# Attention stage of a gated block written out instead of looped, with another opening, maxima over partitions by TensorE, and earlier weight loads

## The reference

```python
x = x + tanh(g_xattn[0]) * xattn(layernorm(x), ctx, ctx, w_q, w_k, w_v)   # causal, 8 x (1024 x 1024), width 512
x = x + tanh(g_ffn[0])   * ffn(layernorm(x), W1, b1, W2, b2)              # gelu, 512 -> 2048 -> 512
# xattn: softmax(mask((x w_q)(ctx w_k)^T / sqrt(512))) (ctx w_v)
# ffn:   W1 and W2 are ternary: clip(round(w / mean|w|), -1, 1)
```

## Time and profile before

| what | value |
|---|---|
| median of 3 runs | 1773.81 us (1772.19 to 1775.87) |
| profiled execution, own time | 1774.8 us |
| its span in the trace | 1773.0 us |
| PE busy | 1651.3 us (93%) |
| DVE busy | 863.9 us (49%) |
| ACT busy | 658.1 us (37%) |
| POOL busy | 304.0 us (17%) |
| mean granted TensorE clock | 0.97 of 2.4 GHz |

### The profile page before, as it was taken

How to read it: one execution, slowest core, us unless ns; L and a number is a source line. 1 busy time by engine, 2 the same in 40 slices (tenths; PEclk the granted TensorE clock), 3 DMA queues, 4 the chain that set the end, 5 groups by cost and what they waited for, 6 DMA issues and landing times.

```text
span 1773.0 us, 24221 instructions
## 1 busy us (share of the span) xinstructions
PE 1651.3 (93%) x8448; PEld 826.3 (47%) x8448; DVE 863.9 (49%) x1575; ACT 658.1 (37%) x1032; POOL 304.0 (17%) x339
## 2 busy tenths in 40 slices
PE   4699999999999988777699999999999999999999
PEld 1355555565555544433244444444444444444444
DVE  3655656565566554546334434444444444444432
ACT  1223232424233343321244444444444444444443
POOL 1111111111111111111021112211122111221110
PEclk8799999999999998988899999999999999999999
DMA  5245463545545375454322211222112222122210
GB/s 184 71 100 143 98 144 94 138 102 134 104 94 150 90 203 151 131 143 106 82 49 65 66 59 33 61 65 65 59 25 69 65 62 62 24 71 62 64 41 24
DMA packets 261651, 157.52 MB, mean 89 GB/s; under 512 B 222416, under 2 KB 222416, under 8 KB 260432
## 3 DMA queue, kind: packets, MB, share of 16 engines
q1 hardware_dynamic: 261008, 156.31, 34.0%
q10 hardware_dynamic: 576, 0.27, 0.1%
HBM read 70.53 MB, written 33.55 MB: 59 GB/s over the span
## 4 chain that ended last, share of the span: by engine, by line
PE 63%; issue 13%; DVE 12%; DMA 4%; SPq 3%; ACT 3%; POOL 1%; DVEq 0%; POOLq 0%; ACTq 0%
PE t_ps L848 13%; PE e_ps L942 12%; PE s_ps L942 12%; PE v_ps L848 11%; PE o_ps L917 5%; PE s_ps L868 4%; PE t_ps L887 3%; PE v_ps L905 3%; DMA w_in<-in_w1T 2%; SPq L277 2%; DVE v_s L811 2%; DVE cmax L592 2%; DVE negmax L677 1%; ACT p_s L460 1%; DVE w_s L759 1%
## 5 line engine op out<-in xcount | busy, mean ns | idle before, releaser
L785 DVE SCALAR_TENSOR_TENSOR v_s<-g,sc,v_s 128x512 f16<-128x512 f32 x256 | 247.6, 968 | 467.5 <-ACT v_s L517 464.0
L942 PE MATMUL e_ps<-w_s,v_s 128*128 128x512 f16 x1024 | 265.5, 379 | 0.8
L942 PE MATMUL s_ps<-w_s,v_s 128*128 128x512 f16 x1024 | 262.8, 379 | 0.0
L848 PE MATMUL v_ps<-ctx_s,w_s 128*128 128x512 f16 x1024 | 243.6, 381 | 8.9 <-DVE w_s L759 8.9
L848 PE MATMUL t_ps<-ctx_s,w_s 128*128 128x512 f16 x1024 | 243.2, 380 | 0.0
L905 PE MATMUL v_ps<-wv_s,ctx_s 128*128 128x512 f16 x768 | 192.5, 404 | 51.3 <-DVE v_s L719 43.2
L868 PE MATMUL s_ps<-ctx_s,tT 128*128 128x512 f16 (+3 forms) x1152 | 202.3, 331 | 21.4 <-DVE tT L697 14.2
L917 PE MATMUL o_ps<-v_s,pT 128*128 128x512 f16 x864 | 199.9, 383 | 5.0 <-DVE v_s L719 5.0
L887 PE MATMUL t_ps<-xnT,a_s 128*128 128x256 f16 x1536 | 183.5, 277 | 22.6 <-ACT a_s L500 18.6
L517 ACT ACTIVATE v_s<-g,sc 128x512 f16<-128x512 f32 x256 | 184.6, 721 | 8.3
L455 ACT ACTIVATE p<-s_ps,ebias,esc 128x128 f32<-128x128 f32 (+3 forms) x64 | 53.1, 830 | 339.5 <-DVE ebias L683 339.5
(11 more groups left out here) (89 smaller groups left out, 1238.4 us busy)
## 6 DMA issues: line engine op xcount, KB each, us to landing
x_ring<-in_x SPq DMA_DIRECT2D x64, 256.0 KB, 2.8
raw<-in_ctxT SPq DMA_DIRECT2D x8, 2048.0 KB, 8.0
out_y<-x_ring SPq DMA_DIRECT2D x64, 256.0 KB, 2.2
raw<-out_y SPq DMA_DIRECT2D x64, 256.0 KB, 3.2
out_y<-v_s SPq DMA_DIRECT2D x64, 256.0 KB, 2.1
w_in<-in_w1T SPq DMA_DIRECT2D x16, 512.0 KB, 4.3
w_in<-in_w2T SPq DMA_DIRECT2D x16, 512.0 KB, 4.6
xnT<-xn_s SPq DMA_TRANSPOSE x128, 2.5
```

The costliest lines, as they stand in the source:

```text
L785: v.scalar_tensor_tensor(out=g_s[:, f % 4, LO], in0=g32[:, f % 2], scalar=col(C_SG), in1=g_s[:, f % 4, HI], op0=ALU.mult, op1=ALU.subtract ...
L848: last_mm = mm(h_ps[f % 2], w1_s[:, c, (f % FC) * P:(f % FC + 1) * P], yT[:, (f // FC) % 2, a, c, :], start=(a == HI and c == 0), stop=(a ...
L942: last_mm = mm(y_ps[i], g_s[:, f % 4, a, i * P:(i + 1) * P], w2_s[:, f, :], start=(f == 0 and a == HI), stop=(f == FC - 1 and a == LO))
```

## The change

- The `Fori` over three attention turns becomes a Python loop on every engine: 64 slots one behind the other, with no branch. The MLP keeps its loop.
- Maxima and sums over partitions: DVE writes the column of maxima on a diagonal (`ident` times the column, into `dg`), PE multiplies it with ones (`spread_ctx`, a float32 matmul), and DVE reduces the row in PSUM. For the context this matmul stands in PE's slot i = 3, between the scores and T.
- The opening is in another order. Loads go by two queues, A's scale comes from a bound on the weights, known before A is done, PE does ten matmuls ahead of the product, both first T products go to two banks, and the rows of tiles 2 to 4 come later.
- In DVE's slots the lower half of V comes before the output of the tile before, and a second ternary step lies between the two.
- Weight loads of slot t+1 are issued in slot t. `W_PLAN` begins with "SS" and ends sums in slot NT-9, and the sums over partitions move to slots NT-13 and NT-9.
- MLP: four banks for hidden chunks instead of two, PE three chunks ahead. The first three hidden chunks need only W1.

```diff
+            def spread_ctx(batch):
+                pe.wait_ge(ctx_diag, batch + 1)
+                mm(MAXES[:, 0:P], ones[:, :], dg[:, 0], start=True, stop=True).then_inc(ctx_max_all, 1)
...
                     last_mm.then_inc(s_mm, 1)
+                if s > 0 and ctx_step(s) == 3 and (not last or t + TB < NT):
+                    spread_ctx(it * 2 + s // TB + 1)
...
+            def ctx_diagonal(batch):
+                dve.wait_ge(ctx_max, batch + 1)
+                v.scalar_tensor_tensor(out=ccol[:, :], in0=cmax[:, 0:1], scalar=TINY, in1=cmax[:, 1:2],
+                                       op0=ALU.max, op1=ALU.max).then_inc(ctx_col, 1)
+                dve.wait_ge(ctx_col, batch + 1)
+                v.tensor_scalar(dg[:, 0], ident[:, :], ccol[:, :], None, ALU.mult).then_inc(ctx_diag, 1)
...
                         if c == 2:
                             ins.then_inc(ctx_max, 1)
+                            ctx_diagonal(batch)
...
-                if reduce_ctx:
-                    g.partition_all_reduce(call[:, :], cmax[:, :], P, RMAX).then_inc(ctx_max_all, 1)
...
-            with pe.Fori(0, TURNS - 1) as it:
+            for it in range(TURNS - 1):
...
-        W_PLAN = {NT - 15: "SSS", NT - 14: "SSS", NT - 13: "SSS", NT - 12: "SS", NT - 11: "TS", NT - 10: "TS",
-                  NT - 9: "TS", NT - 8: "TS", NT - 7: "TS", NT - 6: "TT", NT - 5: "TT", NT - 4: "TT", NT - 3: "TT",
-                  NT - 2: "TT", NT - 1: "T"}
+        W_PLAN = {NT - 15: "SS", NT - 14: "SSS", NT - 13: "SSS", NT - 12: "TSS", NT - 11: "TSS", NT - 10: "TSS",
+                  NT - 9: "TSS", NT - 8: "T", NT - 7: "T", NT - 6: "T", NT - 5: "T", NT - 4: "TT", NT - 3: "TT",
+                  NT - 2: "TT", NT - 1: "TT"}
...
-                        if at == t:
+                        if at == t + 1:
                             load_weights(m)
...
-                    pe.wait_ge(w_ternary, NW)
+                    pe.wait_ge(w_ternary, NW // 2)
                     hidden(0, 0, 0)
                     hidden(1, 1, 0)
+                    hidden(2, 2, 0)
...
+            t_product(0, -2)
+            t_product(0, -1)
+            spread_ctx(0)
+            v_product(0, -1)
+            slot(0, 0)
```

More of the change, by code:

```diff
@@ L203, in gated_block @@
         PV0 = 2
+        O0 = 1
         def p_turned_by(it, s):
@@ L305, in _ @@
             sp.sem_inc(pv_mm, PV0)
+            sp.sem_inc(o_done, O0)
             sp.sem_inc(y_done, GT)
@@ L432, in _ @@
             a = nc.scalar
+            for c in range(DC):
+                act.dma_start(wqk_in[:, 1, c], wkT[:, c]).then_inc(w_qk_in[c], 16)
+            act.dma_start(wv32, wv).then_inc(w_v_in, 16)
             act.dma_start(col(C_G0), g_xattn.partition_broadcast(P)).then_inc(small_in, 16)
@@ L702, in slot @@
                 for m, n in terns[:1]:
+                    ternary(m, n)
+                if not last or t + 1 < NT:
+                    v_lower(it, s)
+                for m, n in terns[1:]:
                     ternary(m, n)
@@ L738, in slot @@
                                     ALU.add).then_inc(w_total, 1)
-                for m, n in terns[1:]:
-                    ternary(m, n)
             def ternary(m, n):
@@ L826, in _, with product @@
             mm = nc.tensor.matmul
-            def product(c):
-                pe.wait_ge(w_qk_in[c], 32)
-                for m in range(DC):
+            def product(m, cs):
+                for c in cs:
+                    pe.wait_ge(w_qk_in[c], 32)
                     last_mm = mm(a_ps[m], wqk_in[:, 0, c, m * P:(m + 1) * P], wqk_in[:, 1, c, :],
                                  start=(c == 0), stop=(c == DC - 1))
-                    if c == DC - 1 and m % 2:
-                        last_mm.then_inc(a_mm, 1)
+                return last_mm
             def hidden(F, f, g):
@@ L855, in slot @@
                 i = s % TB
-                if s >= 0 and (not last or t < NT):
+                if not last or t < NT:
                     par, pr, q = (s // TB) % 2, (s // 2) % 2, s % 2
@@ L908, in slot @@
+                if not last or t + 1 < NT:
+                    v_product(it, s)
                 if s >= 1:
                     pe.wait_ge(p_turned[(s - 1) % 2], p_turned_by(it, s - 1))
-                    pe.wait_ge(v_split, t + 1 if not last or t < NT else NT)
-                    if last and t == NT:
-                        pe.wait_ge(o_done, NT - 1)
+                    pe.wait_ge(v_split, t)
+                    pe.wait_ge(o_done, t + O0 - 1)
                     jn, par = (s - 1) % TB, ((s - 1) // TB) % 2
@@ L919, in slot @@
                     last_mm.then_inc(pv_mm, 1)
-            for s in range(FIRST_SLOT, 1):
-                slot(0, s)
-                for c in PRODUCTS.get(s, ()):
-                    product(c)
-            with pe.Fori(0, TURNS - 1) as it:
+            pe.wait_ge(consts, 1)
+            for _ in range(WARM):
+                mm(m_ps[:, 0:P], ones[:, :], ones[:, :], start=True, stop=True)
+            for c in range(2):
+                for m in range(DC):
+                    product(m, (c,))
+            for m in range(DC):
+                product(m, (2, 3)).then_inc(a_mm, 1)
+                if m == 0:
+                    pe.wait_ge(a_bound, 1)
+                    mm(BOUND, ones[:, :], wbound[:, :], start=True, stop=True).then_inc(a_bound_all, 1)
+            pe.wait_ge(w_diag, 2)
+            mm(MAXES, ones[:, :], dg[:, :, :].rearrange("p w n -> p (w n)"), start=True,
+               stop=True).then_inc(wmax_all, 1)
+            t_product(0, -2)
+            t_product(0, -1)
+            spread_ctx(0)
+            v_product(0, -1)
+            slot(0, 0)
+            for it in range(TURNS - 1):
                 for s in range(1, BODY + 1):
@@ L934, in group @@
                     F = g * FC + f
-                    if not last or F + 2 < NG * FC:
-                        hidden(F + 2, gg * FC + f + 2, g + (f + 2) // FC)
+                    if not last or F + 3 < NG * FC:
+                        hidden(F + 3, gg * FC + f + 3, g + (f + 3) // FC)
                     pe.wait_ge(g_split, F + 1)
```

374 lines of the change are left out of this document (216 added, 158 removed).

## The result

The changed kernel takes 1701.3 us (median of 4 runs, 1697.72 to 1706.45), and the kernel before takes 1773.0 us beside it (4 runs, 1769.67 to 1775.87). The ratio is 0.9598 [0.9568, 0.9629], so it is faster by 71.7 us. The forecast was 1698 us, in 1658 to 1736. The profiled execution took 1701.67 us, its span is 1699.5 us, and the mean granted clock is 0.985.

What follows compares the result with a forecast made beforehand. PE was taken to bound the MLP and the middle, with the opening and last turn loose. 1774.8 - 74 - 0.5 + 21 - 1 - 7 - 14 = 1699.3, forecast as 1698 us, range 1658 to 1736.

Steps and rivals of the forecast that it cites:

- The last turn, -74: Slot 49's scores to first hidden chunk: waits for weight chunks go, 241.6 us becomes 167.5; bounds -35 and -78.
- the spread's 5.6: In the last turn, the context maximum's spread by TensorE stalls PE once, 5.6 us.
- my 163 to 175: Expected sign: scores of tile 49 to first hidden chunk take 163 to 175 us at clock 0.97 or more.
- The middle, +21 - 1 - 7: Slots up to 48: maximum by TensorE costs five batches +21 us, first batch gains 1, unrolled seams gain 7.
- The 1.4 for POOL's part: In each batch, POOL's reduction no longer delays rows, T and V in slots i = 5 and 6: 1.4 us saved.
- The loop's seams, -7: At 263.54 and 447.01, PE's waits of 2.61 and 2.91 us and 1.3 us of clock go when unrolled.
- The opening, -14: Up to 99.39 us: A's scale known earlier, T waits only for transposed rows; -14 us, bounds -5 and -23.
- The MLP, 0: In the MLP, PE had 5 us of idleness in 902, so four banks bring 0.
- the seam, -0.5: Seam to the MLP: three hidden chunks ahead of the last output instead of two, -0.5 us, bounds -3 and +3.
- the first rival: At the maxima: DVE is early enough, no stall, 1660 us; chance 0.17.
- the second rival: In the last turn: DVE takes over, half of the term goes, +37, 1735 us; chance 0.2.
- the third rival: In the 48 formerly looped slots: straight code must be fetched, 2.6 to 2.9 us each, 1830 us; chance 0.04.

Runs made afterwards that it cites:

- late loads: Changed kernel with each weight load issued again in the slot that uses it: 1765.35 us, ratio 0.9949.
- early loads alone: Kernel before with one edit, the weight loads of slot t+1 issued in slot t: 1722.04 us, ratio 0.97.
- the matmul's new place: Changed kernel with PE's `spread_ctx` moved from ahead of T to behind V in the same slot: 1677.45 us, ratio 0.9439.

## Why the prediction was right, and where its terms were off

The total was 3 us off, and that it was so near is luck in part, because two errors of the sum cancel: the last turn gave 9 us less than its term and the MLP with its seam 7 us more.

- **The last turn, -74.** It was -64.65, inside the bounds. The mechanism is shown from both sides (late loads, early loads alone). The mis-sized step is "I leave 4 us of waits for PE": with the spread's 5.6 that made 9.6 us over the bare work of 157.9, and it was 19.05. PE waited 2.32 us at the spread, 2.17 for the sums, 4.12 for T behind the MLP's rows, 1.01 with no engine named, and 2.81 for the output of tile 62, in sum 12.4, and the rest is mostly slower matmuls behind them. The spread's own share was less than its 5.6, for behind its 2.32 us T took 2.78 and lost no clock. I had looked for what DVE does in its slots, not for what stands in its queue from the next stage. The stage missed my 163 to 175 by 2 us. The second ternary instruction, 1.94 us in the mean against 1.33, some 10 us of DVE in all, was not in my sum either.
- **The middle, +21 - 1 - 7.** It was +13.25 against +13. The stall was right: 3.9 forecast, 3.85 in the mean of the five batches, one of them (4.75) over my upper bound of 4.3. So was its size with clock. A batch of the changed kernel takes 94.57 us and one with no wait 88.6, which makes 6.0 for the wait and its clock, that I had put at 3.9 + 1.5 = 5.4. The matmul itself is in both batches; my 3.9 was "with the matmul" already, so the 0.25 counted it twice. The 1.4 for POOL's part fits too: 90.2 less 88.6 is 1.6. Two edits worked on the stall: the matmul's new place took it away (24 us), and the old place of V's split shortened it (12 us).
- **The loop's seams, -7.** No issue wait was left in the middle. With the loop back the middle took 11.95 us more by the traces, in an execution that is the slowest of its four, and the whole kernel 5.7 to 8.7 us more by the timed runs. The waits themselves are 5.8 of it and the slower scores behind them 1.6. The waits for the diagonal were 1.4 us longer too, 20.6 against 19.3, and the T behind them slower by 1.6; why is open.
- **The opening, -14.** It was -14.96, and T started at 26.75 us, close to the earliest that I gave (26.12). Behind it stand two more waits, ahead of T of slots 0 and 2:

```profile
26.75 4.45 PE L947 MATMUL t_ps<-xnT,a_s 128*128 128x256 f16 x24 [3.05 <-issue]
...
50.60 4.76 PE L947 MATMUL t_ps<-xnT,a_s 128*128 128x256 f16 x24 [8.61 <-issue]
...
71.97 4.33 PE L947 MATMUL t_ps<-xnT,a_s 128*128 128x256 f16 x24 [3.80 <-issue]
```

The profile puts them down to no engine. They stand where the code waits for the transposed rows of tiles 2 to 5, which fits "rows 2 to 4 are now normalised after T", but no run moves these rows back. Apart from the ten matmuls, which brought nothing, as forecast, the opening's parts were not tried by themselves.
- **The MLP, 0, and the seam, -0.5.** The MLP's first output matmul starts 13.39 us behind the first hidden chunk before (884.15) and 13.36 after (817.76), but by then four chunks are done instead of three. A chunk takes 1.73 us, so for equal work the seam gave -1.8 and the rest -5.4. The step that failed is "the MLP had 5 us of idleness in 902, so four banks bring 0". I read PE's idle time alone; with the MLP's edits undone 6.7 us came back behind the first hidden chunk, and 17.6 us of waits of its weight loads. So what there was to gain stood in these waits and within what counts as busy.
- **The rivals.** The stalls came, seven of them, so the first rival fell. DVE did not take over the last turn, though a quarter of what the second rival feared (9 of 37 us) came, as single waits. Straight code brought no waits spread over the slots: the third rival fell.

## What to carry to other kernels

The wait to remove is the one at the head of the chain: one condition on when loads are issued brought 53 us, more than everything else of this change together, and it shows in a profile as waits of a slack engine for a DMA, with the bound engine waiting for that engine. When a matmul is put in for work of another engine, look where its input is ready before you place it; two places further back in the queue it cost 24 us less. And read the weight loads' waits beside the matmuls' own: an engine that looks 99% busy may still have 0.6% to give.

## What the hardware showed beyond that

**Two engines in each other's way.** In the last turn of the changed kernel, the ternary instruction and POOL's two instructions for rows stand side by side, in the timeline:

```profile
755.00 2.28 DVE L815 SCALAR_TENSOR_TENSOR w_s<-w_in,sc,g 128x1024 f16<-128x1024 f32 x1
755.05 1.16 POOL L389 TENSOR_TENSOR xn_s<-xn,xn_s 128x512 f16<-128x512 f32 x1 [3.18 <-ACT xn_s L477]
756.16 2.25 POOL L401 TENSOR_TENSOR raw<-raw,b_row 128x512 f32<-128x512 f32 x1
```

Alone, DVE's takes 1.28 us, and L401 takes 1.27 in the median of its 64. The lengths fit turns taken one behind the other: POOL works until 756.21, DVE's 1.28 us are over some 1.1 us later, at 757.28, and POOL's second needs until 758.41, 1.13 us more. The Trainium skill (SBUF — State Buffer, SBUF: two separate sides) says that a DVE instruction with two SBUF inputs and a GpSimd one that reads SBUF share a port pair as an exclusive lock for the whole instruction. The rows agree: POOL's first one keeps the 1.16 us that it takes in the median, so it gave nothing up to DVE's. What they don't explain is that DVE's is recorded 0.05 us ahead of it and still waits, and no run here tries the order of the two starts.

**The clock after a short wait.** PE waits of 2.04 and 2.05 us were followed by slower matmuls (5.11 us against 3.43), and one of 2.04 us at the same slot of another kernel was not. Of two waits of 1.90 us ahead of the same matmul, in one execution, one was followed by T in 4.45 us and one by T in 2.78. A wait of 3.36 us was followed by T in 2.78 us in the kernel with the MLP as before (271.85 us, granted clock 1.00), and one of 3.36 us in the kernel without the ten matmuls by T in 4.45 (174.19 us). Of the two seams, one of 2.61 us was not the earlier trace rows, and one of 2.66 us with the loop back was. So from 1.9 to 3.4 us the same wait may or may not cost clock, and what decides is open. A stall of such a length should be priced with both ends, here nothing and about 1.7 us or more.
